# Self-attention: V fills and router pieces on TensorE ahead of the scores

## The reference

```
x = layernorm(x + attn(x))          # 4 blocks: linear attention (elu + 1), gelu, feed-forward 512
x = layernorm(x + xattn(x, ctx))    # cross-attention, 16 heads of 8, masked softmax
x = layernorm(x + ffn(x))           # causal self-attention, router, experts
```

```
xn = rmsnorm(x);  q, k, v = xn @ q_w, xn @ k_w, xn @ v_w     # 16 heads of 64, rotary q and k
attn = softmax(causal(q k^T / 8));  ctx = attn v
attn_out = ctx @ o_w + o_b + xn;    an = rmsnorm(attn_out)
aff = softmax(an @ router_w + router_b)                      # 31 experts, top 3
out = shared(an) + sum over the top 3 of gate * expert(an) + an + attn_out
```

## Time and profile before

| | us |
|---|---|
| median of 3 runs (lowest, highest) | 903.26 (901.44, 904.5) |
| span of the profiled execution | 867.6 |
| TensorE matmul busy | 796.4 (92%) |
| VectorE busy | 692.1 (80%) |
| ScalarE busy | 572.9 (66%) |
| GpSimd busy | 562.2 (65%) |

### The profile page before, as it was taken

How to read it: one execution, slowest core, us unless ns; L and a number is a source line. 1 busy time by engine, 2 the same in 40 slices (tenths; PEclk the granted TensorE clock), 3 DMA queues, 4 the chain that set the end, 5 groups by cost and what they waited for, 6 DMA issues and landing times.

```text
span 867.6 us, 17391 instructions
## 1 busy us (share of the span) xinstructions
PE 796.4 (92%) x5325; PEld 525.5 (61%) x5325; DVE 692.1 (80%) x2494; ACT 572.9 (66%) x1445; POOL 562.2 (65%) x638
## 2 busy tenths in 40 slices
PE   5899999999889999999989999999999888989994
PEld 2344444444466676766546676676667556888773
DVE  4788888888788988889878859976995985565786
ACT  3588778777489999999656647645664656355334
POOL 4888888888662333232377749665788988663773
PEclk9799999999989999999999999999999999999997
DMA  8300000000015011100222222221222236264112
GB/s 242 116 2 0 1 1 0 1 0 1 0 36 153 30 42 56 39 1 2 50 65 68 65 50 51 68 65 40 63 76 77 54 93 195 91 191 146 50 49 61
DMA packets 57851, 51.88 MB, mean 60 GB/s; under 512 B 11586, under 2 KB 43042, under 8 KB 57762
## 3 DMA queue, kind: packets, MB, share of 16 engines
q1 hardware_dynamic: 55394, 46.05, 19.2%
q0 software_dynamic: 2304, 4.72, 1.9%
q10 hardware_dynamic: 64, 0.02, 0.0%
HBM read 21.66 MB, written 12.32 MB: 39 GB/s over the span
## 4 chain that ended last, share of the span: by engine, by line
PE 51%; POOL 19%; DVE 13%; issue 8%; ACT 7%; ACTq 0%; DVEq 0%; POOLq 0%
PE psum L2199 5%; PE psum L2028 4%; PE psum L2061 4%; POOL area L970 4%; DVE area L1482 4%; PE psum L2355 3%; PE psum L2336 3%; PE psum L2394 3%; PE psum L2258 3%; PE psum L2045 3%; POOL area L879 3%; PE psum L2087 3%; PE psum L2372 3%; POOL slot_in L958 2%; PE psum L1912 2%
## 5 line engine op out<-in xcount | busy, mean ns | idle before, releaser
L970 POOL TENSOR_TENSOR area<-area,rinv 128x512 f32<-128x512 f32 x64 | 94.2, 1472 | 64.7 <-DVE rinv L1803 64.3
L1275 ACT ACTIVATE area<-area,negmax 128x128 f32<-128x128 f32 (+1 forms) x256 | 112.8, 444 | 17.7 <-DVE negmax L1482 17.4
L1122 ACT ACTIVATE area<-area,negmax 128x256 f32<-128x256 f32 x256 | 108.9, 507 | 0.2
L1470 DVE SCALAR_TENSOR_TENSOR area<-psum,ccol,cs 128x512 f32<-128x512 f32 x128 | 89.4, 740 | 21.2 <-PE psum L2061 21.0
L1482 DVE CUSTOM_DVE_ANT_0 area<-psum,area 128x256 f32<-128x256 f32 x256 | 93.2, 420 | 14.4 <-PE psum L2013 13.9
L1482 DVE CUSTOM_DVE_ANT_0 area<-psum,maskc 128x128 f32<-128x128 f32 (+1 forms) x256 | 75.8, 351 | 10.0 <-PE psum L2087 10.0
L2028 PE MATMUL psum<-ident,area 128*128 128x128 f32 x512 | 70.9, 279 | 9.0 <-DVE area L1522 7.7
L2061 PE MATMUL psum<-area,qkw 128*128 128x512 f32 x128 | 71.9, 643 | 6.3 <-DVE area L1470 4.5
L2028 PEld LDWEIGHTS psum<-ident,area 128*128 128x128 f32 x512 | 57.3, 143 | 18.1 <-issue 11.3
L1265 ACT ACTIVATE area<-psum 128x512 f32<-128x512 f32 x32 | 19.1, 598 | 72.1 <-PE psum L2394 72.0
L2372 PEld LDWEIGHTS psum<-ident,area 128*128 128x128 f32 x384 | 44.8, 141 | 35.2 <-issue 24.9
(11 more groups left out here) (308 smaller groups left out, 2092.3 us busy)
## 6 DMA issues: line engine op xcount, KB each, us to landing
area<-area SPq DMA_DIRECT2D x256, 64.0 KB
slot_out<-area SPq DMA_DIRECT2D x17, 256.0 KB, 2.4
area<-slot_in SPq DMA_DIRECT2D x8, 512.0 KB, 4.0
slot_in<-gate SPq DMA_DIRECT2D x5, 768.0 KB, 4.6
area<-in_L_ffn_re_w SPq DMA_DIRECT2D x14, 256.0 KB, 3.4
area<-in_mask_BxSxS_ik SPq DMA_DIRECT2D x8, 256.0 KB, 3.8
area<-in_L_attn_W SPq DMA_DIRECT2D x5, 256.0 KB, 6.2
area<-in_x SPq DMA_DIRECT2D x4, 256.0 KB, 3.4
```

The costliest lines, as they stand in the source:

```text
L970: pool.tensor_tensor(p4, p4, rinv[:, u % 4, 0:4].unsqueeze(2).to_broadcast([128, 4, w]), ALU.mult)\
L1122: last = act.activation(P[:, n % 4, r, mm, :], P[:, n % 4, r, mm, :], ACT.Exp, bias=negmax[:, n % 4, r, mm:mm + 1], scale=-1.0)
L1275: last = act.activation(Pc[:, u % 4, r, mm, 0:w], Pc[:, u % 4, r, mm, 0:w], ACT.Exp, bias=negmax[:, u % 4, r, mm:mm + 1], scale=-1.0, accu ...
L1470: last = nc.vector.scalar_tensor_tensor(rp[:, w, j, :].rearrange("p (b n) -> p b n", b=2), src.rearrange("p (b n) -> p b n", b=2), ccol[:, ...
```

## The change

TensorE's step `u` was: `half` fill, transposes of `u - 1`, scores of `u + 2`, all spare pieces except `half`, `out`, `rank`, `base`, then values of `u - 2`. Now the spare pieces come ahead of the scores. VectorE's step was: reciprocal, `half` read, copy, maxima of `u + 2`, reads of spare pieces. Now `v`, `logits`, `pick`, `b2` and three tail pieces are read ahead of the maxima; `out`, `rank` and `base` stay behind them. ScalarE, GpSimd and the DMA queue keep their order, and no instruction is added or removed.

```diff
@@ VectorE, self_attention
                     if u == 1:
                         read_spare(g, steps[0], following)
+                    for step in steps:
+                        if step[0] in ("v", "logits", "pick", "b2") or step[0] == "tail" and step[1] in ("tokens0", "tokens1", "out"):
+                            read_spare(g, step, following)
                     if u < SU and (u + 2 < SU or following is not None):
                         self_max(g, u + 2)
                     for step in steps:
-                        if step[0] in ("v", "out", "logits", "rank", "base", "pick", "b2") or step[0] == "tail" and step[1] in ("tokens0", "tokens1", "out"):
+                        if step[0] in ("out", "rank", "base"):
                             read_spare(g, step, following)
@@ TensorE, self_attention
                     if u == 1:
                         fill_spare(g, steps[0], following)
-                    if u < SU and (u + 2 < SU or following is not None):
-                        self_scores(g, u + 2)
                     for step in steps:
                         if step[0] not in ("half", "out", "rank", "base"):
                             fill_spare(g, step, following)
+                    if u < SU and (u + 2 < SU or following is not None):
+                        self_scores(g, u + 2)
                     if 2 <= u < SU + 2:
                         values(u - 2)
```

## The result

| | before | after |
|---|---|---|
| median, us | 904.12 (16 runs, 899.74 to 908.75) | 908.55 (16 runs, 903.99 to 911.32) |
| ratio, 95% interval | | 1.0044 (1.003 to 1.0058) |
| profiled execution: time, span | span 867.6 | 907.37, 905.6 |

The change costs 0.44%, 4.0 us. I had forecast 903.3 us in a range to 907.0 and "no change" as the likeliest. The prediction was wrong.

The account below looks back on a forecast made before the run. TensorE was taken to bound groups 0 to 2 and GpSimd group 3. Terms -1.4, +0.6 and +0.9 gave +0.1 us on the span of 867.6; with 35.7 around it, 903.3 us, range 897.0 to 907.0.

Parts of the forecast that it names:

- no change: Outcome within 0.3% (2.7 us) of the kernel before, given chance 0.5.
- The saving of 0.19 us a unit: TensorE, groups 0 to 2: cheaper tile-shape switches, 0.09 on transposes and 0.10 on V fills; 33 units, at most 6.3 us.
- What the change costs: Step pricing waits now ahead of scores: `rms` in group 0, `turn` and L1707 in groups 1 and 2, `gates` in group 1.
- sum of waits: Savings and waits together: group 0 gains 1.4, group 1 loses 0.6, group 2 loses 0.9; in all +0.1 us.
- `rms`, `turn` and `gates`: TensorE waits: `rms` +0.64 and 0.38 savings lost; `turn` waits 0.7, next `half` 0.3 late; `gates` waits 2.6, `half` 1.3 late.
- The held subtraction: VectorE L1707, unit 5, groups 1 and 2: comes after GpSimd's rotation has begun, is held, makes VectorE 0.87 us late.
- Group 2 and 3: Group 2 loses 0.9, its savings in units 10 to 15 not counting; group 3, paced by GpSimd, changes by 0.
- The span and 35.7 us around it: Whole kernel: median 903.26 lies 35.7 us above the profiled span of 867.6, taken as unchanged.
- Late maxima, the slower rival: Later scores delay maxima, exponentials, reciprocal and GpSimd's normalisation: 0.6 in each of 10 V units, 6 us, 909.3; chance 0.1.

Follow-up runs that it names:

- e2: The kernel before with only the V fills moved ahead of the scores, and VectorE's reads likewise; 902.36 us, ratio 0.9983.
- e5: The whole change plus unneeded repeats of the scores on TensorE ahead of `rms` in group 0 and `gates` in group 1; 870.93 us against 869.86, ratio 1.0013.
- e9: The whole change timed and profiled again, no edit; 911.72 us against 908.46, ratio 1.0033.
- e6: The whole change with only `turn` put back behind the scores on TensorE; 867.78 us, ratio to before 0.9975.
- e7: The whole change with only `gates` put back behind the scores on TensorE; 872.49 us, ratio to before 1.0035.
- e11: The whole change, but with `rms`, `turn` and `gates` behind the values on TensorE; 904.67 us, ratio to before 0.9965.
- e1: The kernel before, timed and profiled again, no edit; 904.31 us, ratio 0.9997, span 902.4.
- e4: The whole change with `rms`, `turn` and `gates` put back behind the scores on TensorE, VectorE's order as changed; 899.62 us, ratio to before 0.995.
- e8: The whole change with only `rms` put back behind the scores on TensorE; 872.35 us, ratio to before 1.0022.
- e10: TensorE's half of the change alone, VectorE in the order of the kernel before; 913.34 us, ratio to before 1.0054.
- e12: Same kernel as e4, run again on the chip of e11; 905.05 us against 908.46, ratio 0.9964.

## Why the prediction was wrong, point by point

**The saving of 0.19 us a unit: right in size, over-counted by two.** Units with a V fill ahead of the scores show it in groups 0 and 1 and the first half of group 2, nearly all of them; e2 ends group 2 with 2.3 us of it (-0.60 to -2.88 of shift), less than the whole since `rms` and `gates` take up what was gained just ahead of them. In group 0 I had counted 13 units; in e5 eleven gained, and units 1 and 12 gave nothing (-0.14 and -0.15 at steps 1 and 2, and 1.06 at `rms`, which leaves no saving of its own). That is 0.4 us: group 0 gained 1.0 there, for my 1.4. The Trainium skill, TensorEngine Tiling (Array Packing), Key Properties, says that changing the tiling mode drains TensorE; the trace agrees in sign, and 0.19 us is what two changes fewer are worth here.

**The step that failed: "What the change costs" priced each wait at its own length and the clock at full speed throughout.** The granted clock in the earlier trace rows was 1.00, and I carried it over to a kernel whose waits I had myself forecast longer. They came out as forecast: 0.64 us at `turn` (0.7 predicted), 2.59 at `gates` (2.6), 1.76 at `rms` (the 0.73 of before, 0.64 and 0.38 make 1.75); the `half` behind `gates` started at 554.62 (554.5). What I left out is that TensorE then runs at half speed for about 3 us. This cost 1.6 us at each place (2.67 against 1.06, 3.17 against 1.58), 3.2 in all. The change itself shows the second without any added matmul: in e9 it waits the same 2.59 us at `gates`, the clock stays up, and `gates` costs 1.58. With e5's busy waits group 2 ends 0.17 late, 0.3 less its offset, where my sum said 0.1. The ratio of e5, 1.0013, against 1.0044 and 1.0033 of the change on other chips points the same way outside the trace. So the sum of waits was right to 0.2 us, with some luck (in e5 group 0 gained 0.4 less than I had said, groups 1 and 2 lost 0.1 less each), and the missing term is the clock.

**It does not fall every time.** In the 14 traces, `rms` and the `gates` of group 1 give 28 waits. After those of 1.76 to 2.59 us the clock fell in 7 of 12 cases: for 1.76 at `rms`, in the change, e6 and e9 but not in e7; for 2.59 at `gates`, in the change but not in e9. After waits of 0.69 to 1.38 it fell in none of 14; the other two, in e11, were 0.53 and 0.64. So the cost of a moved piece that waits longer is a chance, not a sum.

It falls at other places too, and there shorter waits stand ahead of it. Near 443 all 14 traces have the same wait of 1.57 or 1.58 us, and the clock fell behind it in 3: e1, which is the kernel before, the change and e9. At the `turn` of group 3 it fell in 2 of 6 where the wait is 1.47 or 1.48 as before (e1 and e4), and in 6 of 7 where `turn` has moved and waits 2.11 or 2.12. One more place where the change makes TensorE wait longer costs time by the clock: `rank` of group 2. TensorE is idle ahead of its small bf16 matmuls for 1.31 us in the change and 0.19 before, and 0.41 more behind them. The clock fell there in e7, e8 and e9, not in e5 or the first trace of the change, which have the same waits. From e9:

```profile
629.52 0.27 PE L2276 MATMUL psum<-area,below 128*128 128x248 bf16 x1 [1.31 <-issue]
...
630.86 2.07 PE L2064 MATMUL psum<-area,qkw 128*128 128x512 f32 x2 [0.41 <-DVE area L1470]
```

It costs 1.2 us (2.34 against 1.11 in the table). The two traces of the change lose nearly the same up to the end of group 2 (3.5 and 3.1 us), since each has two such falls besides the one near 443, at `rms` and `gates` in one and at `rms` and `rank` in the other. The same may be why e7 and the whole change are alike in time; no run separates that. The Trainium skill, TensorE: Matmul & The Clock Gate, Part 1, says that at the start of a kernel the number of matmuls ahead of the clock's rise varies from run to run; for a fall in mid-kernel, e9 beside the first trace of the change shows such a difference.

**`rms`, `turn` and `gates`: right in place, wait and direction,** each within 0.1 us where the clock stayed up.

**The held subtraction: right in time, wrong in its cause.** L1707 took 1.17 us and `gates` came 0.89 later than in the earlier trace rows, for my 0.87. But I laid it to VectorE's new order. e4 and e6 keep that order, and it takes 0.43 to 0.45; e10 has the old order and `gates` comes just as late, 1.20 on the shifted scale. `turn` ahead of the scores makes the maxima late, and whatever VectorE does first, the subtraction then ends with the rotation. The rule that I had cited from the Trainium skill, SBUF — State Buffer, Who interferes with whom, agrees with both traces (the subtraction ends within 0.2 us of the rotation's end); what it did not decide is how late `gates` comes.

**`turn` was under-sized.** I gave it 0.1 a group after `logits` had given back its part. Through the subtraction it also sets when `choose` ends, and so how long TensorE waits at `gates` and in group 2. Put back alone, it gives 0.9975, where the whole change has 1.0033 and 1.0044 on other chips. By its trace against the change's: 0.5 at `turn` itself and 2.3 at `gates` in group 1, of which 1.6 is the clock, 0.5 and 0.7 in group 2.

**Group 2 and 3.** I had 0.9 lost in group 2; e5 lost 0.81. For group 3 I had 0, and the change lost 0.13 from step 1 to 16. e5 lost 1.08 there: near 711, where the kernel before has one stretch at half speed too, e5 has two in a row (clock 0.52, 0.50 and 0.84 in the windows of 3 us from 710 on, against 0.59, 0.84 and 1.00).

**"The span and 35.7 us around it": wrong.** The time of a profiled execution is its span and 1.8 us (907.37 and 905.6). The first profile of before was of an execution some 34 us shorter than those timed. It did no harm to the sum, which lies in the stage where the traces agree to 0.05 us.

**Late maxima, the slower rival: refuted.** It gave 909.3, near the time measured, for a reason that is not there. The late maxima show as longer waits of ScalarE (17.4 us in the first profile of before, 27.0 and 24.6 below), and the reciprocals wait as often as before. Waits from 445 to 742 in the change, and in the faster e4 (waiter, line, us, times, longest):

```profile
POOL area L970 <- DVE rinv L1803: 72.5, 32, 8.2
ACT area L1275 <- DVE negmax L1482: 27.0, 23, 3.6
DVE rinv L1803 <- ACT area L1275: 10.2, 3, 5.7
```

```profile
POOL area L970 <- DVE rinv L1803: 64.6, 28, 8.2
ACT area L1275 <- DVE negmax L1482: 24.6, 22, 3.6
DVE rinv L1803 <- ACT area L1275: 10.2, 3, 5.7
```

ScalarE waits 25 to 27 us for maxima in both, and one of them is faster than before. The third row is that of the earlier trace rows with the 8 us stall of e1 in it: 3 times again.

**What stays open.** What ends ScalarE's long waits at the border of groups 2 and 3 and in the expert stage, in the profiles of e1 to e4 and e9 to e12 and of the change, but not in the first profile of before and in none of e5 to e8, which shared the chip where before took 869.86; and whether it can be told beforehand if the clock falls after a given wait.

## What to carry to other kernels

When pieces are moved ahead on an in-order engine, move those that never wait and leave those that do where their wait is shortest: here that gives 0.9964 and 0.995 of the kernel before, while moving all pieces loses 0.3 to 0.4%. Before pricing a longer wait on TensorE, look in several traces of the kernel for waits of that length and how often the granted clock fell behind them, and count the slow stretch as a term of its own, with that chance. One trace may not show it: the first profile of before has full speed behind its wait of 1.58 us, the second has not. And ask of each piece what a late result does two units on: `turn` cost little where it stood and most where `gates` waited.

## What the runs showed of the hardware that I had not expected

The granted clock fell to half after TensorE waits of 1.48 and 1.58 us in the kernel before (second profile, at the `turn` of group 3 and near 443), and stayed up after one of 2.59 (e9); the same wait of 1.76 did either. A stretch at half speed cost 1.6 us at `rms` and at `gates`, nearly as much as the wait of 1.76 ahead of the first. Filling most of the wait of 2.59 us with 24 MATMUL instructions for nothing took that cost away (1.58 of shift at `gates` instead of 3.17). And a VectorE instruction that reads two operands from SBUF ends with GpSimd's rotation whether it starts 0.3 or 0.9 us after that has begun (1.17 and 0.52 us long), so putting it earlier bought nothing.
